# Feed table ahead of the slot list, and row fetches exchanged between SyncE and GpSimd, in a fused two-block vision tower

## What is computed

```python
x = hidden_states.reshape(-1, h)                      # 832 x 256
shared_out = silu(x @ sgw) * (x @ suw) @ sdw          # every token
logits = x @ gate_w                                   # 32 experts
topk_ids = argmax(logits); scores = sigmoid(max(logits))
sorted_x = (x * scores)[argsort(topk_ids)]
d = ragged(silu(ragged(sorted_x, gate)) * ragged(sorted_x, up), down)
out = h + shared_out + d[inverse order]
```

## Time and profile before

| | us |
|---|---|
| median of 3 runs (lowest to highest) | 349.75 (349.19 to 349.86) |
| the profiled execution | 351.12 |
| its span | 349.4 |
| TensorE matmul busy | 303.4 (87%) |
| VectorE busy | 206.2 (59%) |
| ScalarE busy | 135.3 (39%) |
| GpSimd busy | 53.4 (15%) |
| transferred | 67.99 MB, mean 195 GB/s |

### The profile page before, as it was taken

How to read it: one execution, slowest core, us unless ns; L and a number is a source line. 1 busy time by engine, 2 the same in 40 slices (tenths; PEclk the granted TensorE clock), 3 DMA queues, 4 the chain that set the end, 5 groups by cost and what they waited for, 6 DMA issues and landing times.

```text
span 349.4 us, 6673 instructions
## 1 busy us (share of the span) xinstructions
PE 303.4 (87%) x2484; PEld 216.5 (62%) x2484; DVE 206.2 (59%) x590; ACT 135.3 (39%) x309; POOL 53.4 (15%) x74
## 2 busy tenths in 40 slices
PE   1996979668899999999995899989899899996965
PEld 1775547558799999999874566665345334552331
DVE  0355593332646556556347589975973899635653
ACT  1012141422422322422404456636434976505641
POOL 0111000001111101101000010110532002111853
PEclk9999898959999999999999599999999999997888
DMA  7999992000651641540947600000188999999641
GB/s 288 396 436 426 410 309 80 2 0 1 242 189 56 239 173 68 182 156 26 356 160 296 273 2 4 1 9 0 49 286 292 386 349 363 348 380 369 89 62 31
DMA packets 13290, 67.99 MB, mean 195 GB/s; under 512 B 1754, under 2 KB 7466, under 8 KB 9162
## 3 DMA queue, kind: packets, MB, share of 16 engines
q1 hardware_dynamic: 11178, 64.41, 49.0%
q0 software_dynamic: 2080, 3.15, 4.5%
HBM read 61.52 MB, written 6.04 MB: 193 GB/s over the span
## 4 chain that ended last, share of the span: by engine, by line
PE 69%; DVE 11%; DMA 10%; issue 4%; ACT 3%; POOL 2%; ACTq 0%; SPq 0%; DVEq 0%; POOLq 0%
PE P L346 15%; PE P L454 8%; PE P L466 8%; DMA arena<-experts_dram 7%; PE P L634 7%; PE P L583 5%; PE P L380 4%; PE P L490 4%; PE P L442 2%; PE P L647 2%; PE P L516 2%; PE P L531 2%; DMA arena<-patches_dram 2%; DVE arena L999 1%; ACT arena L812 1%
## 5 line engine op out<-in xcount | busy, mean ns | idle before, releaser
L346 PE MATMUL P<-arena 128*104 128x256 f32 x288 | 74.4, 399 | 9.5 <-DMA arena<-patches_dram 7.2
L346 PEld LDWEIGHTS P<-arena 128*104 128x104 f32 x288 | 47.7, 177 | 22.8 <-issue 8.4
L1297 POOL TENSOR_TENSOR rstd<-var,mhalf 104x1 f32<-104x1 f32 x40 | 22.0, 550 | 213.7 <-DVE var L922 213.7
L634 PE MATMUL P<-arena,cols 128*32 128x512 f32 x288 | 36.7, 654 | 4.2 <-ACT cols L853 3.6
L828 ACT ACTIVATE arena<-arena 128x1024 f32 x31 | 31.6, 1051 | 16.2 <-SPq L331 11.3
L466 PE MATMUL P<-arena 128*128 128x104 f32 x256 | 29.9, 275 | 2.4 <-ACT arena L768 2.4
L466 PEld LDWEIGHTS P<-arena 128*128 128x128 f32 x256 | 29.7, 192 | 3.1 <-issue 1.4
L454 PEld LDWEIGHTS P<-arena 128*128 128x128 f32 x256 | 30.8, 197 | 1.3 <-issue 0.7
L454 PE MATMUL P<-arena 128*128 128x104 f32 x256 | 30.7, 279 | 0.5 <-issue 0.5
L768 ACT ACTIVATE arena<-P,arena 128x104 f32<-128x104 f32 x64 | 17.0, 348 | 28.7 <-PE P L454 28.7
L634 PEld LDWEIGHTS P<-arena,cols 128*32 128x32 f32 x288 | 9.2, 119 | 25.4 <-issue 19.2
(11 more groups left out here) (203 smaller groups left out, 493.5 us busy)
## 6 DMA issues: line engine op xcount, KB each, us to landing
arena<-experts_dram SPq DMA_DIRECT2D x22, 1536.0 KB, 7.7
arena<-experts_dram SPq DMA_DIRECT2D x8, 2048.0 KB, 12.3
arena<-patches_dram SPq DMA_DIRECT2D x4, 624.0 KB, 6.5
sorted_x<-arena SPq DMA_DIRECT2D x1, 2184.5 KB, 36.1
arena<-shared_dram SPq DMA_DIRECT2D x1, 1536.0 KB, 32.0
arena<-w_dram SPq DMA_DIRECT2D x1, 1024.0 KB, 10.0
out_dram<-arena SPq DMA_DIRECT2D x1, 1024.0 KB, 34.0
out_dram<-h POOLq DMA_DIRECT2D x8, 104.0 KB, 5.9
```

Of the source, the lines that this page charges most:

```text
L346: last = mm(P[b][0:a.shape[1], col:col + D], a, rhs(c), start=(c == 0), stop=(c == chunks - 1))
L634: last = mm(P[b][part, :], xT[:, c, part], weights(u)[:, c * INNER:(c + 1) * INNER], start=(c == 0), stop=(c == DC - 1), tile_position=(0, ...
L1297: nc.gpsimd.tensor_tensor(rstd[:, :], var[:, :], mhalf[:, :], ALU.pow).then_inc(s["rstd_ready"], 1)
```

## The change

- VectorE works out the feed table first and copies it out; the slot list is made behind it, between and after the copy. `hidden(1)` stands inside the feed chain.
- TensorE transposes the feed table between the two halves of `shared_up(3)`, not after it.
- SyncE no longer waits for the sorted rows and no longer fetches the windows of the fixed quads. It goes from the first two expert transfers into its loop, with a semaphore (`rounds_ready`) for the number of rounds. Behind that loop it has a new one that fetches the row blocks of the loop's quads.
- GpSimd fetches the three windows after its scatters, ahead of the eighth quad's rows, and no later row blocks.
- The third shared down product goes ahead of the first quad (SHARED_FIRST 2 to 3).
- `more` is read before the fixed quads on TensorE, ScalarE, VectorE and GpSimd.
- In the loop the gate and the up weights have semaphores of their own, and the result is evacuated after the gate copies.

```diff
-SHARED_FIRST = 2
-SHARED_AT = ((), (), (), (2,), (3, 4), (5, 6, 7), (), ())
+SHARED_FIRST = 3
+SHARED_AT = ((), (), (), (), (3, 4), (5, 6, 7), (), ())
...
 SyncE
             feed(entry(0), 0)
             second = entry(1)
             feed(second, 1)
-            sp.wait_ge(xs_sent, 16 * GROUPS)
-            for i in range(len(WINDOW_PARTS)):
-                window(i)
+            sp.wait_ge(s["rounds_ready"], 1)
             feeds = sp.value_load(table[0:1, T_FEEDS:T_FEEDS + 1], min_val=1, max_val=FEEDS)
...
+            sp.wait_ge(s["table_ready"], 1)
+            more = more_quads(sp)
+            with sp.Fori(0, more) as i:
+                sp.wait_ge(s["l_xt_done"], i + 1)
+                sp.wait_ge(s["l_aim_ready"], i + 1)
+                sp.dma_start(xw[:, STILL, :], sorted_x[bass.ds(i * 128 + (STILL + 1) * 128, 128), :]).then_inc(l_rows_in, 16)
...
 TensorE
-            for n in range(2, 4):
-                shared_up(n)
-            pe.wait_ge(s["feeds_ready"], 1)
...
+            shared_up(2)
+            shared_up(3, feed_entries)
             shared_up(4)
...
             with pe.Fori(0, more) as i:
-                pe.wait_ge(l_window_in, 16 * (i + 2))
+                pe.wait_ge(l_rows_in, 16 * (i + 1))
...
+                pe.wait_ge(s["l_upw_in"], 2 * (i + 1))
                 strips(2, up_of).then_inc(s["l_up_done"], 1)
...
 VectorE
-            link(V.tensor_tensor(big[:, :, :], P[4][0:GT, 0:256].rearrange("p (g e) -> p g e", e=EXPERTS), onehot_b[:, :, :], ALU.mult))
...
-            V.tensor_copy(slot_i[:, :], slot).then_inc(s["slot_ready"], 1)
-            hidden(1)
...
+            hidden(1)
...
             V.tensor_scalar_add(tcol[:, 4:5], own[:, 0:1], 1.0).then_inc(s["feeds_ready"], 1)
+            link(V.tensor_tensor(big[:, :, :], P[4][0:GT, 0:256].rearrange("p (g e) -> p g e", e=EXPERTS), onehot_b[:, :, :], ALU.mult))
+            V.tensor_tensor_scan(rt[:, 3, :], rt[:, 2, :], rt[:, 7, :], 0.0, ALU.add, ALU.add)
+            link(V.tensor_reduce(rank, big[:, :, :], AX.X, ALU.add))
+            dve.wait_ge(s["feeds_done"], 1)
+            V.tensor_copy(table[:, 0:T_QUAD], P[5][0:1, 288:288 + T_QUAD]).then_inc(s["feeds_table"], 1)
...
+            V.tensor_copy(slot_i[:, :], slot).then_inc(s["slot_ready"], 1)
...
 GpSimd
             pool.wait_ge(xs_sent, 16 * GROUPS)
+            for i, q in enumerate(WINDOW_PARTS):
+                end = (WINDOW_PARTS + (STILL,))[i + 1]
+                pool.dma_start(xw[:, q:end, :], sorted_x[q * 128:end * 128, :].rearrange("(r p) c -> p r c", p=128)).then_inc(windows_in[i], 16)
...
-                if r == STILL - 1:
-                    pool.wait_ge(s["l_xt_done"], 1)
-                    window(STILL + 1)
...
-                pool.wait_ge(s["l_xt_done"], i + 2)
-                pool.wait_ge(s["l_aim_ready"], i + 1)
-                window(i + (STILL + 2))
```

More of the change, by code:

```diff
@@ L194, in tower @@
                  "l_xt_done l_xT_ready l_gate_done l_up_done l_sgate_ready l_hw_ready l_ht_done l_hT_ready l_dn_done l_y_ready "
-                 "aim_ready l_aimed l_aim_ready l_added l_gatew_in l_target_ready l_turn stored").split()
+                 "aim_ready l_aimed l_aim_ready l_added l_gatew_in l_upw_in l_target_ready l_turn stored").split()
         s = {n: sem(n) for n in names}
@@ L573, in logits, with shared_up @@
                 last.then_inc(s["lg_done"], 1)
-            def shared_up(n):
+            def shared_up(n, between=None):
                 m, half = n // 2, n % 2
@@ L584, in shared_up @@
                                   start=(c == 0), stop=(c == DC - 1))
+                    if between and b < 2:
+                        between()
                 last.then_inc(s["sg_done"], 1)
@@ L607, in _, with feed_entries @@
             last.then_inc(s["prefix_done"], 1)
-            for n in range(2, 4):
-                shared_up(n)
-            pe.wait_ge(s["feeds_ready"], 1)
[L611 to L614, removed]
+            def feed_entries():
+                pe.wait_ge(s["feeds_ready"], 1)
+                entries = P[5][0:1, 288:288 + FEED * EXPERTS].rearrange("p (n i) -> p n i", i=FEED)
+                for i in range(FEED):
+                    last = mm(entries[:, :, i], tcol[0:EXPERTS, 2 + i:3 + i], ident[0:EXPERTS, 0:EXPERTS], start=True, stop=True)
+                last.then_inc(s["feeds_done"], 1)
+            shared_up(2)
+            shared_up(3, feed_entries)
             shared_up(4)
@@ L674, in next_xt @@
                 xt(q).then_inc(s["xt_done" if q < STILL else "l_xt_done"], 1)
+            more = more_quads(pe)
             next_xt(0)
@@ L859, in silu_gate @@
                 return A(sg, P[0][:, :], ACT.Silu)
+            more = more_quads(act)
             act.wait_ge(s["xt_done"], 1)
@@ L1119, in _ @@
             V.tensor_scalar(rt[:, 5, :], count, 1.0 / STRIP, (STRIP - 1) / (2.0 * STRIP), ALU.mult, ALU.add)
-            link(V.tensor_tensor(big[:, :, :], P[4][0:GT, 0:256].rearrange("p (g e) -> p g e", e=EXPERTS), onehot_b[:, :, :], ALU.mult))
[L1121 to L1125, removed]
-            link(V.tensor_reduce(first, big[:, :, :], AX.X, ALU.add))
-            link(V.scalar_tensor_tensor(slot, first, float(STRIP), rank, ALU.mult, ALU.add))
-            V.tensor_copy(slot_i[:, :], slot).then_inc(s["slot_ready"], 1)
-            hidden(1)
             at_k = route[:, C_K:C_K + 1]
@@ L1136, in _ @@
             link(V.tensor_scalar(used, count, 0.0, None, ALU.is_gt))
+            V.tensor_scalar(rt[:, 2, :], rt[:, 5, :], ROUND, ROUND, ALU.add, ALU.subtract)
             link(V.tensor_tensor_scan(visits, used, rt[:, 7, :], 0.0, ALU.add, ALU.add))
@@ L1223, in _ @@
             dve.wait_ge(s["table_ready"], 1)
+            more = more_quads(dve)
             need, where = weights_of(dve, 0)
@@ L1261, in _ @@
                         need, where = weights_of(dve, q + 2)
-            more = more_quads(dve)
+            nc.vector.nop().then_inc(s["l_aim_ready"], 1)
             nc.vector.nop().then_inc(s["l_y_ready"], 1)
@@ L1327, in _ @@
             pool.wait_ge(s["table_ready"], 1)
+            more = more_quads(pool)
             for r in range(STILL):
```

34 lines of the change are left out of this document (13 added, 21 removed).

## The result

| | before | change |
|---|---|---|
| median of 4 runs, us | 349.81 (349.19 to 352.25) | 355.47 (354.20 to 357.56) |
| the profiled execution, and its span | 351.12, 349.4 | 354.20, 352.3 |
| TensorE / VectorE / ScalarE / GpSimd busy | 303.4 / 206.2 / 135.3 / 53.4 | 302.0 / 206.2 / 135.2 / 53.1 |
| expert transfers, median to landing | 7.7 | 8.3 |

The ratio is 1.0152, with an interval of 1.0111 to 1.0193: the change is **slower by 1.5%**, and lies above the range of the forecast. The two profiled executions are only 2.9 us of span apart, because the change's is the quickest of its four runs and before's is 1.3 us above its median. What follows compares the profiles with each other, and the medians with each other.

A forecast was written before the change was run, and what follows sets the result against it. The prediction took GpSimd's queue of final adds to bound the kernel. First strips 5.2 us later, less 7.0, made the span 347.6, 1.8 under 349.4; applied to the median 349.75 it forecast 348.1, range 346.0 to 351.3.

The forecast's parts named there:

- the copies' hold: GpSimd's last three scatters, held by VectorE's weight copies: 1.3 us taken, between bounds of 0 and 2.6.
- So q=5 starts 5.2 − 1.8 = 3.4 later.: TensorE's sixth quad: delayed 5.2 us by late rows, less 1.8 for the third shared product moved ahead.
- These move by d; so the twelfth lands near 317 as now.: Expert transfers: seventh and eighth follow copies shifted by d, yet the twelfth lands near 317 and q=6 starts near 319.
- d: Shift of TensorE's first strips against 268.17, through later sorted rows: forecast 5.2 us, strips at 273.4.
- The first add starts at 326.0.: GpSimd's scatter-adds at the end: the first starts at 322.56 + 3.4 = 326.0.
- The adds end the program: End of the kernel: GpSimd's unbroken adds finish last, the final one landing at 344.8, span 347.6.
- in good time: SyncE's fetch of the loop's rows: TensorE's 2.75 us wait goes, its last result there at about 338.
- a sign that it was wrong: GpSimd's last add waiting for TensorE, which would mean that the adds did not bound the end.
- the change is d − 7.0: Rule for the whole span: the first strips' shift less 7.0 us, giving 1.8 less than 349.4.
- the fair case: Rival "Fair sharing", at the scatters' landing: they land at 266.6 with nothing held, d about 3, 346.0 us; chance 0.14.
- 271.9 for the landing after all four transfers: Upper bound for the scatters' landing, if their queue gets its turn only after four expert transfers; 268.2 was taken.
- Rows starved: Rival: scatters land only after all four expert transfers, d 8.9, span 351.3, median 351.6, slower; chance 0.25.

The follow-up runs named there:

- e5: The change run again unaltered, against the kernel before: 356.10 us, ratio 1.0155.
- e14: The change run once more unaltered, on another chip, against the kernel before: 354.89 us, ratio 1.0133.
- e6: The change with SyncE waiting for the scatters before its loop, GpSimd still fetching the windows: 350.21 us, 0.9985 of before.
- e1: The change with the slot list made before the feed table again, windows still fetched by GpSimd: 350.63 us, 0.9987 of before.
- e10: e2 with an early release of SyncE's row fetch and the third shared product back in its old place: 347.98 us, 0.9860 of before.
- e8: e2 with the third shared product back in its old place: 348.44 us, 0.9965 of before.
- e3: The change with SyncE waiting for the scatters and fetching the windows, slot list still late: 351.25 us, no ratio.
- e2: e1 with SyncE waiting for the scatters and fetching the windows: 347.79 us, 0.9872 of before.
- e11: The change with VectorE's release of SyncE's row fetch moved early, into the first quad: 353.55 us, 1.0058 of before.

## Why the prediction was wrong, step by step

The first half came out, in part by luck. The first scatter is 251.07 against 246.91 before, so the slot list was 4.2 later; 4.9 was forecast, but the change's whole routing runs 0.8 earlier in this profile, so that step was right. The first transfer left at 250.75 (251.6). The scatters had landed at about 268.5 (268.2), the window at 272.36 (272.3), the first strips started at 273.31 (273.4). But two terms behind the landing were off and cancelled with the early routing. From the end of the last scatter's issue to the landing the forecast had 4.9 us (263.35 to 268.2), less than the 6.8 that it took before beside two transfers; it measured 6.7. And the copies' hold came out smaller than the 1.3 taken: of the last three scatters one took 1.27 and two 1.04, against 0.99 unheld, some 0.4 in all. By the Trainium skill (SBUF — State Buffer, SBUF: two separate sides) an fp32 copy of VectorE shuts GpSimd out of its port until the copy ends; these rows show no scatter held for a whole copy.

Four steps behind the first strips failed.

1. **"So q=5 starts 5.2 − 1.8 = 3.4 later."** It was 5.0: the first strips ran at a granted clock of 0.50 and cost 1.6 more. The forecast put TensorE's wait down as free cover for the third product; 2.3 us of it were left behind the product by its own times, 3.52 in the profile, and it left out what the engine does when it comes out of such a wait. All three profiles of the change have it (5.23 to 5.34). The row for it was there: 6.47 us for the strips after 3.08 us idle.
2. **"These move by d; so the twelfth lands near 317 as now."** The two halves contradict each other. The eighth transfer moved by 6.85 (5.1 and the slow strips), and from it on the transfers follow one another to the end. 5.2 of this was left at the twelfth, which left at 312.50 against 307.31 and landed at 322.25; q = 6 started at 324.72, not 319, and q = 7 at 333.86. The product moved out of the way (1.8) does not help here: it stood behind the eighth transfer's start, and counted for q = 5 alone.
3. **"The first add starts at 326.0."** It was 328.55: 1.6 from the first step, and 1.0 because the last store took 8.9 us from its issue to the add, where it took 7.9. This second part did not repeat (6.9 in e5, 7.7 in e14); its cause is not shown.
4. **"The adds end the program", and SyncE fetches "in good time".** SyncE's fetch was issued at 339.57, since it waits for a release that VectorE gives only behind the fixed quads; TensorE waited 1.92 us for it. With q = 7 late as well GpSimd waited 2.29 us for the last result, which the forecast had named as a sign that it was wrong. Both waits are in all three profiles (TensorE 1.92 to 1.98, GpSimd 2.29 to 4.30); in e5 the seventh add waited too, 1.42 us. The last add started at 345.34 and not 340.8: 2.4 for the late row of adds (step 3 less a little), 2.3 for this wait, less 0.2 for the step between them.

Of span these make 4.7 us: 347.6 forecast, 352.3 measured; from the start of the routing it is 5.5. As the sum above has it, the rule "the change is d − 7.0" should have been d + 1.7 − 3.9.

Two smaller slips stand in the forecast's numbers: the fair case and nine tenths of 0.45 are 0.55, not 0.56, and its 271.9 for the landing after all four transfers is not worked out, where the sum before it gives 270.7. Neither matters for what failed.

Of the rivals none came. "Rows starved" had the right sign and a right reason, that software-queued transfers wait behind the expert transfers, but at d = 8.9 and by the same wrong rule. The forecast put the rows' delay down to the late slot list (+4.2) and only 0.4 to the fourth transfer; e6, with the slot list as late, has its first strips at 270.16, so some 3 us of d = 5.1 came from the missing wait. The late list was the other half: with it put back (e1) the loss was gone too. Fair sharing had 0.14. The Trainium skill (DMA: Bandwidth & Descriptors, Queues, rings and completion order) has each DMA engine change between its queues by packets; the window load of 2.1 to 2.4 us with the transfers held back and 7.4 beside two of them speaks against a fair share by time, and says nothing on the size of the packets that take turns.

The forecast also took the span difference for the time difference. The medians are 5.7 us apart, the profiles' times 3.1. Of the other 2.6 us one half is that before's profile is above its median, the other that the change's is below. What makes the runs of one kernel differ goes with the clock: on the chip of e5 before took 348.3 to 349.6 us in the five runs whose mean granted clock was 0.957 to 0.962, and 350.3 to 353.0 in the six with 0.944 to 0.951; of the change's six runs the quickest (353.8) had 0.955 and the others 0.945 to 0.947. Which waits make the difference is not shown.

## What to carry to other kernels

A wait that seems to idle a queue may be what keeps large transfers off the path of small ones: before it goes, ask what stands behind it in its queue and whether that can be used any earlier. Here the two transfers that it let through filled places whose weights nobody wanted yet, and the next could not start before the quads that they had delayed. In a ring of buffers follow the chain from the first use to the transfer that refills it. From the first strips to the eighth transfer it was 22.0 to 22.1 us in ten of the sixteen profiles, 22.5 in e6, 22.9 in e10, and 23.7 to 23.8 in the four whose first strips took 5.2 to 5.3 us: a shift of the first use comes back at the refill. What of it reaches the end is another question (5.2 of 6.85 at the twelfth transfer here, nothing of e8's 2.2).

## What the runs showed of the hardware

- A 128.5 KB load took 2.1 us (SyncE, e3) or 2.4 us (GpSimd, e6) with the expert transfers held back, 3.1 before, 3.6 in the change beside the end of one, and 7.4 in e1 beside two.
- How long TensorE waits does not alone settle its clock. Strips after waits of 1.9 us (e1), 2.7 us (e14, q = 7) and 2.8 us (e6, q = 6) took 3.64 us; after 2.0 us (e10, q = 7), 2.1 us (e2, q = 6) and 2.2 us (e6, q = 7) they took 5.34, 5.34 and 5.24.
- Scatter issues beside VectorE's copies took 1.04 to 1.27 us in the change and up to 1.40 in its variants (e11), 0.99 without: far less than the store of 1.96.
- The kernel before had medians of 349.8 to 352.1 us in five comparisons, with single runs from 348.3 to 354.1. Differences of one per cent needed the comparison on one chip, and some of them more runs than were made.
